# Mixture-of-experts kernel: where the expert weights' loads are issued, and how the last piece of a weight set is converted

## What is computed

```python
x = x + _layernorm(_L0_attn_ref(_layernorm(x), ...))
x = x + _layernorm(_L0_ffn_ref(_layernorm(x), wg, w1, v1, w2))
# _L0_ffn_ref, T = 4096 tokens, E = 32, K = 8, H = 512, F = 192
scores = jax.nn.softmax(x @ wg.T, axis=-1)
weights, idx = jax.lax.top_k(scores, K)
weights = weights / jnp.sum(weights, axis=-1, keepdims=True)
xs = x[t_s]                                   # the rows, sorted by expert
g = jax.lax.ragged_dot(xs, w1, group_sizes)   # 512 -> 192
u = jax.lax.ragged_dot(xs, v1, group_sizes)   # 512 -> 192
h = jax.nn.silu(g) * u
ys = jax.lax.ragged_dot(h, w2, group_sizes)   # 192 -> 512
out = zeros.at[t_s].add(ys * w_s[:, None])
```

## Time and profile before

| | |
|---|---|
| median of 3 runs | 2569.39 us (2566.04 to 2571.1) |
| the profiled execution's own time | 2559.13 us |
| span of its profile | 2557.4 us |
| experts' stage, first to last tile of PE | 1218.8 to 2486.5 us |
| busy over the span: PE, DVE, ACT, POOL | 89%, 62%, 51%, 37% |
| DMA queues, share of 16 engines over the span: q0 (POOL's), q1 (SP's), q10 (ACT's) | 28.1%, 22.2%, 4.1% |

### The profile page before, as it was taken

How to read it: one execution, slowest core, us unless ns; L and a number is a source line. 1 busy time by engine, 2 the same in 40 slices (tenths; PEclk the granted TensorE clock), 3 DMA queues, 4 the chain that set the end, 5 groups by cost and what they waited for, 6 DMA issues and landing times.

```text
span 2557.4 us, 66537 instructions
## 1 busy us (share of the span) xinstructions
PE 2268.8 (89%) x11804; PEld 1933.1 (76%) x11805; DVE 1580.1 (62%) x4955; ACT 1293.3 (51%) x2786; POOL 953.4 (37%) x1126
## 2 busy tenths in 40 slices
PE   7999899999989999982898898978999888988990
PEld 5887588888868888861777887867889777977880
DVE  4455567777767777763555666655666555655446
ACT  3343556566556666641445555544555454545443
POOL 1112025555535555554233333323334233323342
PEclk9999999999999999995899999989999899989995
DMA  3233113332333333335997777767777676766777
GB/s 116 92 116 113 58 34 126 112 126 104 129 125 124 109 121 117 108 122 181 256 236 156 151 144 154 144 153 154 143 146 140 150 155 141 140 147 132 136 130 287
DMA packets 162140, 353.33 MB, mean 138 GB/s; under 512 B 20640, under 2 KB 20640, under 8 KB 161952
## 3 DMA queue, kind: packets, MB, share of 16 engines
q0 software_dynamic: 60224, 144.21, 28.1%
q1 hardware_dynamic: 90816, 173.06, 22.2%
q10 hardware_dynamic: 11040, 35.40, 4.1%
HBM read 173.46 MB, written 179.14 MB: 138 GB/s over the span
## 4 chain that ended last, share of the span: by engine, by line
PE 30%; issue 7%; DMA 5%; DVEq 3%; ACTq 3%; DVE 3%; ACT 2%; POOL 1%; SPq 0%; POOLq 0%
PE bank L449 5%; PE bank L450 5%; PE bank L451 5%; DMA moe_sum<-X,aidx 4%; PE bank L438 3%; PE bank L466 2%; PE bank L459 2%; PE bank L470 2%; PE bank L468 2%; PE bank L467 2%; PE bank L469 2%; ACTq L324 2%; DVEq L723 1%; ACT BIG L591 1%; DVE WB L607 1%
## 5 line engine op out<-in xcount | busy, mean ns | idle before, releaser
L1471 POOL DMA_INDIRECT moe_sum<-X,aidx x274 | 429.3, 1567 | 877.3 <-issue 636.5
L951 PE MATMUL bank<-WB,XH 128*128 128x512 f32 x1536 | 479.0, 393 | 0.0
L449 PE MATMUL bank<-WB,XL 128*128 x1096 | 400.5, 365 | 16.8 <-DVE WB L607 9.4
L450 PE MATMUL bank<-WB,XH 128*128 x1096 | 374.2, 341 | 0.0
L451 PE MATMUL bank<-WB,XH 128*128 x1096 | 373.1, 340 | 0.0
L951 PEld LDWEIGHTS bank<-WB,XH 128*128 128x128 f32 x1536 | 290.8, 189 | 60.2 <-issue 0.5
L951 PE MATMUL bank<-WB,XL 128*128 128x512 f32 x768 | 316.5, 412 | 11.1 <-DVE XL L1258 11.1
L723 DVE SCALAR_TENSOR_TENSOR BIG<-BIG,bank x274 | 95.1, 347 | 362.3 <-ACT BIG L518 305.2
L951 PE MATMUL bank<-WB,SH 128*128 128x512 f32 x1024 | 319.0, 393 | 0.0
L1537 POOL DMA_INDIRECT sorted_rows<-srow,pos x256 | 266.1, 1039 | 95.2 <-issue 95.2
L518 ACT ACTIVATE BIG<-bank x274 | 91.1, 333 | 406.2 <-PE bank L451 254.0
(11 more groups left out here) (211 smaller groups left out, 4539.3 us busy)
## 6 DMA issues: line engine op xcount, KB each, us to landing
BIG<-sorted_rows SPq DMA_DIRECT2D x276, 274.0 KB
X<-x_in SPq DMA_DIRECT2D x64, 256.0 KB, 2.8
RAW<-w_in ACTq DMA_DIRECT2D x15, 768.0 KB, 4.5
LATE<-w_in ACTq DMA_DIRECT2D x15, 768.0 KB
sorted_rows<-BIG SPq DMA_DIRECT2D x33, 274.0 KB, 4.0
moe_sum<-LATE SPq DMA_DIRECT2D x34, 256.0 KB, 3.0
LATE<-x_in SPq DMA_DIRECT2D x32, 256.0 KB, 3.0
RAW<-wo_in SPq DMA_DIRECT2D x16, 512.0 KB, 3.2
```

Source lines behind the costliest of these rows:

```text
L449: nc.tensor.matmul(eu[s][:, 0:UP], XL[:, s, k, :], wh, start=k == 0, stop=False)
L450: nc.tensor.matmul(eu[s][:, 0:UP], XH[:, s, k, :], wh, start=False, stop=False)
L951: last = nc.tensor.matmul(ps, w, m, start=start and i == 0, stop=stop and i == len(terms) - 1)
L1471: nc.gpsimd.indirect_dma_start(acc_dram[:, :], bass.IndirectOffsetOnAxis(aidx[:, s:s + 1], 0), rows, None, compute_op=ALU.add).then_inc(s_ ...
```

## The change

Four things change in the experts' stage.

1. SP, not ACT, issues `load_weights`, in a loop over experts that it now has too. It enters expert e when it has issued the row loads up to four tiles ahead (`AHEAD = 4`); there it writes the padding page of e + 6, waits for `s_elo`, issues the weights of e + 3, in the first 14 experts one `load_x2`, and then n row loads.
2. A row load now also waits until the row load before it has landed; one semaphore serves both buffers.
3. `load_weights` has a fourth DMA: the last 64 rows of w2 are loaded into both halves of the partitions. ACT scales the fifth piece by -1 in partitions 0 to 63 and by +1 in the others, and DVE takes `raw * keep - high` with `keep` 0 and 1, over all 128 partitions. Both closing loops now run from `min(n, 4)` to 5, one instruction for n of 4 and more. The end of a set on DVE is told by a small copy of its own (`all_low`).
4. ACT waits for the landed weights in front of each piece in the tile loop, no longer at the start of the expert. POOL sets up `sign` and `keep` with four small memsets before the stage.

```diff
-        def each_expert(eng, row, ready, body):
+        def each_expert(eng, row, body, rounds=((0, EXPERTS // WSETS - 1),)):
...
-                              (to[0:FFN - P, W13 + HID:RAW_N], w2_in[bass.ds(e, 1), P:FFN, :])):
+                              (to[0:64, W13 + HID:RAW_N], w2_in[bass.ds(e, 1), P:FFN, :]),
+                              (to[64:P, W13 + HID:RAW_N], w2_in[bass.ds(e, 1), P:FFN, :])):
...
-            def load_rows(g, s):
+            def load_rows(g):
+                s = g & 1
                 row = sp.value_load(at_tile[0:1, 2, bass.ds(g + 2, 1)], min_val=0, max_val=PAGES * PAGE)
                 sp.wait_ge(s_T, g + 1)
+                stand(sp)
                 sp.wait_ge(s_wr, g + 1)
                 stand(sp)
-                sp.dma_start(xr[:, s, :], sorted_dram[bass.ds(row, P), :]).then_inc(s_ld[s], 16)
+                wait(sp, s_ld, 16 * g)
+                stand(sp)
+                sp.dma_start(BIG[:, at(XR, s, ROW, ROW)], sorted_dram[bass.ds(row, P), :]).then_inc(s_ld, 16)
...
+            sp.wait_ge(s_elo, 1)
+            load_weights(sp, 2, 0)
             sp.wait_ge(s_tabd, 1)
-            fill_pads(0, 0)
-            fill_pads(1, 1)
+            for e in range(AHEAD + 2):
+                fill_pads(e, s_fill0)
...
+            for g in range(AHEAD):
+                load_rows(g)
...
+            def body(e, q, first, n, m, lo):
+                i = q % 2
+                if not isinstance(e, int) or e + AHEAD < EXPERTS:
+                    sp.wait_ge(s_fill[i], (e - i) * 8 + 16)
+                    stand(sp)
+                if not isinstance(e, int) or e + AHEAD + 2 < EXPERTS:
+                    fill_pads(e + AHEAD + 2, s_fill[i])
+                if not isinstance(e, int) or e + 3 < EXPERTS:
+                    sp.wait_ge(s_elo, e + 2)
+                    stand(sp)
+                    load_weights(sp, e + 3, (q + 1) % 2)
+                if lo == 0:
+                    load_x2(e, e)
+                elif isinstance(e, int) and e - WSETS * lo < XRING - 12:
+                    load_x2(e - WSETS * lo + 12, e - WSETS * lo + 12)
+                with sp.Fori(0, n) as k:
+                    load_rows(nc.s_assert_within(first + k + AHEAD, AHEAD, MAX_TILES + AHEAD - 1))
+
+            total = each_expert(sp, 0, body, ((0, 3), (3, 6)))
...
-            def ready(e, q):
-                if not isinstance(e, int) or e + 3 < EXPERTS:
-                    act.wait_ge(s_elo, e + 2)
-                    stand(act)
-                    load_weights(act, e + 3, (q + 1) % 2)
-                if converts(e):
-                    act.wait_ge(s_ewr[q % 2], (e - q % 2) * 24 + 96)
-                    stand(act)
...
                     if converts(e):
+                        act.wait_ge(s_ewr[i], (e - i) * 32 + 128)
                         weights_high(to, i, (k & (LOW_PIECES - 1)) * PIECE).then_inc(s_eh, 1)
...
-                    with act.Fori(m, HIGH_PIECES) as k:
-                        weights_high(to, i, k * PIECE)
+                    with act.Fori(m, PIECES) as k:
+                        weights_high(to, i, k * PIECE, sign[:, bass.ds(k >> 2, 1)])
...
-                    dve.wait_ge(s_el, first + n)
-                    stand(dve)
-                    with dve.Fori(m, LOW_PIECES) as k:
-                        weights_low(to, i, k * PIECE)
-                    last_low(to, i)
+                    with dve.Fori(m, PIECES) as k:
+                        low_or_both(to, i, k)
+                    all_low(e + 2)
```

More of the change, by code:

```diff
@@ L658, in moe_dve @@
             done(nc.vector.scalar_tensor_tensor(tn[0:1, 0, :], tn[0:1, 2, :], 512.0, tn[0:1, 3, :], ALU.mult, ALU.add))
[L659 to L660 removed]
+            done(nc.vector.tensor_scalar(words, tn[0:1, 2, :], float(LOW_PIECES), 32768.0, ALU.min, ALU.mult))
             settled()
[L662 to L663 removed]
+            nc.vector.tensor_tensor(table[:, 0, :], words, tn[0:1, 0, :], ALU.add)
             nc.vector.tensor_copy(pair_n[:, :], odd[0:1, 2:3]).then_inc(s_tabd, 1)
```

134 lines of the change are left out of this document (63 added, 71 removed).

## The result

| | median of 7 runs, us | lowest to highest |
|---|---|---|
| before, same chip | 2568.07 | 2565.72 to 2571.54 |
| the change | 2548.16 | 2545.73 to 2559.18 |

The ratio is 0.9931, 95% interval 0.9919 to 0.9944: 20 us gained where 111 were forecast, and outside the range of 2415 to 2520. The profiled execution has a span of 2547.9 us.

What follows compares the result with a forecast made beforehand. PE was taken to bound the kernel inside experts, 3.89 us a tile. Ordinary starts 44, short experts 62, spreading load_x2 and padding 8 and the start -3 sum to 111 us: 2458 us against the 2569.4 median, range 2415 to 2520.

Steps and rivals of the forecast that it cites:

- The stage and its losses: Experts' stage: 199 us of 1267.7 lost, mostly at stops between experts; only those could be won.
- SP's queue: At ordinary expert starts the fifth tile's row load, behind the weights, comes late: 21 us lost, bounds zero and 51.
- The weights start at 4.4 us: SP issues the weights 4.4 us after the expert's first tile begins on PE, once DVE is done.
- The row load's own data take 1.1: Fifth tile's row load lands 1.1 us after the weights, at 12.7 where PE wants it at 11.7: 1.0 us late.
- That one load waits for the landing of the other costs nothing: Row loads one at a time: no cost, since a tile leaves 3.9 us.
- Short experts: Seven stretches with experts of one or two tiles: 62 of 106 lost us won, 44 stay; bounds 15 and 80.
- DVE's closing loop: End of a weight set on DVE: done at about 1743.3 instead of 1744.45, leaving nothing of 4.9 us per ordinary start.
- Spreading `load_x2` and padding: Expert 1: moving both to once an expert removes most of 10 us lost there: 8 us won, bounds 0 and 10.
- The start: Before the stage: more DMAs and padding waits ahead of the page list and first row: -3 us, bounds +3 and -6.
- The queue as a bound: Rival: row loads behind weights in SP's queue become the bound; slower, 2593 at 6 us late each; chance 0.05.
- POOL's adds: Rival: POOL's wait for landed adds at 28 expert starts comes out, 45 us lost again: 2500; chance 0.15.
- ACT's wait for weights: Rival: SP issues weights late, ACT stops in the tile loop 2 us at all 28 loads: near 2510; chance 0.08.

Runs made afterwards that it cites:

- pads_later: The change with the padding moved behind the expert's first row load, load_x2 staying ahead of it: ratio 0.9777 to the kernel before.
- act_later: The change, but ACT issues the weight loads on its own queue, behind its first tile of an expert: ratio 0.9849 to the kernel before.
- spread_act: The change, but ACT issues the weights in four steps, one behind each of the expert's first four tiles: ratio 0.9836 to the kernel before.
- before_serial: The kernel before, but each row load waits for the landing of the one before it: ratio 0.9998 to the kernel before.
- x2_and_pads_later: The change, with padding moved behind the expert's first row load and load_x2 behind the second, weights still first: ratio 0.9739 to the kernel before.
- act_at_start: The change, but ACT issues the weights ahead of its first tile, as in the kernel before: ratio 0.9988 to the kernel before.
- two_parts: The change, reordered: 768 KB of weights, row load, other 512 KB, row load, padding, load_x2 behind the sixth or last row load: ratio 0.9744 to before.

## Why the prediction was wrong

**The stage and its losses: right.** ACT's 152 us and PE's 87.7 us were what stopped the stage, and both went (6.6 and 20.5, forecast "gone" and below 30).

**The step that failed: "SP's queue", priced at 21 us.** The mechanism was named and its price was wrong twice. The 21 us were for the eleven ordinary starts; in the eleven summed above PE waits 34.9 us for rows, inside the bound of 51 (with `load_x2` 4.1 us each where 3.1 were priced, without it 2.9 where 1.0). For the short experts the sum had nothing for it (the 44 us that stay are DVE's and ACT's); there PE waits 36.8 us. Nor had it the half clock behind each such stop, 1.7 us in expert 7. So the starts got worse by 14 us instead of better by 33. The prediction's own alarm, "if that wait passes 100 us", stood too high: 73.4 us in the whole stage were enough. Two premises fell, both in the one place shown above; of a third it is open whether it cost anything.
- "The weights start at 4.4 us" (its own rows make it 4.1: 1743.3 less 1739.22): they start at 5.5, because the padding is issued ahead of them and reads its table first. The step left out its 274 KB and its issue; moving it and nothing else gave 39 us (pads_later).
- "The row load's own data take 1.1" behind the burst: it was issued 10.7 us after the first tile and took 7.17 us more, so it landed at 17.9 where 12.7, or 14.8 with `load_x2`, was forecast. Adding transfers by bytes, with prices from a trace in which PE stood still during the burst, left out POOL's adds and the other rows on the same engines, which were busy 0.97 of the time. That the adds are the part left out is argued. That the price is one of the burst is shown: it stays with the weights in another queue (act_later, 44.9 us) and goes when they are spread there (spread_act, 0.2).
- "That one load waits for the landing of the other costs nothing": SyncE waited 128.7 us for landings, so the wait is met often now. In before it is free (before_serial), and SyncE is 3 us early there. What it costs PE in the change no run shows: 29.2 of the 128.7 us fall where PE never stopped, and in expert 7 the late row load came behind the other issues, not behind a landing.

The lower bound was argued from PE's 1.2 us of waiting for rows before. That number belonged to a kernel that stopped PE while the weights moved. The stop was also the cover of the transfer.

**The clock: rightly tied to the stops.** It was to rise to 0.98; it is 0.96, since the stops moved and did not go. In x2_and_pads_later it is 0.98 over the stage:

```profile
1215.10:2426.70 1211.60, 1133.08 (x6303) 1007.34 (x6304) 730.12 (x1971) 641.31 (x1426) 423.87 (x271) 0.98 0.77 166
```

**Short experts, 62 us: 11 came.** Late rows (36.8 us) took the place of ACT's stop, and late adds stand in the chain too. DVE's part was priced well: 26 us forecast, and PE waits 18.5 us for the gate in the seven stretches. From the chain of the change in the third short stretch:

```profile
1673.00 8.26 DMA BIG<-sorted_rows
1690.32 6.38 DMA BIG<-sorted_rows
1709.54 7.41 DMA moe_sum<-X,aidx
1717.74 5.33 DMA moe_sum<-X,aidx
```

Of the 44 us said to stay, 18 were for weights that ACT meets before they have landed: it waited 25.8 us in 6 places (18.1 and 7.7), the right kind and size. With padding and `load_x2` moved, the stretches are 36 us shorter than before.

**DVE's closing loop "leaves nothing of the 4.9".** act_at_start shows that these microseconds do nothing while ACT issues at the old place. With the issue on SyncE, PE's wait for the gate was down to 20.5 us, so the step held for the whole change, but which part gave how much is not shown.

**Spreading `load_x2` and padding, 8 us: right** in expert 1 (10 us came), but its cost stood in another place, ahead of the weights at every start.

**The start, -3 us: no such cost.** The stage begins at 1215.7 instead of 1218.8. But before_serial, whose start is that of before, begins its stage at 1215.9, so the 3 us are not a gain of the change either.

**The rivals.** The queue as a bound named the place: it was to turn the change into a loss from 5.1 us late at each load. At the ordinary starts PE stood 3.5 us in the mean, 4.6 in expert 7, so its time was not reached either, but the result lies between it and the forecast. A chance of 0.05 was far too little. POOL's adds: ACT's wait for POOL rose from 86.5 to 120.1 us, where 45 us of time were feared; how much of the time it is, no run shows. ACT's wait for weights came to 25.8 us in 6 places, not 2 us at 28. The rule of the Trainium skill's page "DMA: Bandwidth & Descriptors", section "Issuing engines are not separate DMA queues", that the issuer matters for the issue time alone, gave 2505, nearer to 2548 than my own 2458. The rule itself agrees with act_later; what the use of it left out is that with the issuer the time of the burst moved too.

## What to carry to other kernels

A stall can be the cover of a transfer: before removing it, list which bytes move during it, and ask what share of the DMA engines is free in the pace that follows (here 0.75 was in use inside experts). When loads share one queue, order them by how soon each is needed, and put what is needed late (here the padding, which is wanted only experts later) behind what is needed first: two moves in SyncE's program were worth 49 us, more than twice the whole change. A wait that costs nothing in one kernel may be free only by the slack of the engine that holds it, so measure that slack, here SyncE's 803 us, before adding to it.

The version to use is x2_and_pads_later, 0.9739 of the kernel before; two_parts (0.9744) can't be told from it.

## What the runs showed of the hardware

- A row load of 274 KB took 7.17 us behind padding, 1280 KB of weights and 512 KB more in its own queue, and 8.06 us with the weights in ACT's queue. Without the 512 KB it took 5.62 to 6.43 us in the same queue and 5.62 to 6.07 with the weights in ACT's, three loads each. A separate queue gave it no clearly shorter landing.
- While PE stood for that row load, the DMA engines were busy 0.97 of the time, at 234 GB/s.
- Issuing the four weight DMAs took 2.35 to 2.77 us in the rows of L329 on ACT and SyncE above, and in act_at_start 0.7 us passed from there to ACT's next Silu.
- After a stop of 4.61 us PE did its matrix instructions every 0.32 us instead of every 0.18 for some 3.5 us, at a granted clock of 0.51 (1.2 GHz) where 1.00 (2.4 GHz) was granted before. The tile took 5.60 us (1540.55 to 1546.15) in place of 3.9, 1.7 us on top of the stop. The timeline of PE, two instructions at half clock and two at full:

```profile
1542.09 0.52 PE L467 MATMUL bank<-WB,XH 128*128 x1
1542.41 0.52 PE L465 MATMUL bank<-WB,XL 128*128 x1
...
1544.41 0.35 PE L466 MATMUL bank<-WB,XH 128*128 x1
1544.60 0.34 PE L467 MATMUL bank<-WB,XH 128*128 x1
```
